# Sigmoids of the six newest tiles at steps 11, 13 and 15, the last rows' x loaded late with its bias at the end, a fifth output buffer, and another late order on ScalarE

## The chip, the cores and the metric

The kernel runs on one NeuronCore of a Trainium2 chip. The metric is the device time of one execution in microseconds (us). The kernel before took 541.62 us (median of 3 runs, 540.72 to 543.06).

## The reference

There are four samples of x and k, each 1024 (time) x 1024 (channels) in float32. In the program's terms (`tf` is one number per sample, made from cond by a sigmoid of a sum):

```
decay = exp(-exp(w)) * (0.5 + 0.5 * tf)
ek    = exp(min(k, 30));  ekv = ek * k;  euk = exp(min(u + k, 30))
nf, df = forward scans over time:  a = a * decay + ekv,  b = b * decay + ek
nb, db = the same scans backward
wkv   = sigmoid(x) * (nf + nb - ekv + euk * k) / max(df + db - ek + euk, 1e-8)
y     = wkv * (0.8 + 0.2 * tf)
out   = x + y @ (sign(weight) * mean|weight| per output row).T + bias
```

The key and the value of the recurrence are the same tensor k; x is needed twice, once under the sigmoid and once as the residual of the output.

## The kernel before

**Tiles and steps.** A tile is one sample by 128 channels, turned so that the channels lie on the 128 partitions and time is the free dimension: 4 samples x 8 tiles = 32 tiles. The loop over `n` from 0 to 31 is written once per engine as `step`, and the engines meet through semaphores only (`done(engine, name, n)` waits until operation `name` of tile `n` is complete; operations of one engine run in the order written).

**One tile's way.** SP loads k (L243) and x (L216). TensorE turns k into the PSUM tensor kT (`k_turn`). ScalarE makes the two exponentials (`exps`, L526 and L527). VectorE clamps (L717), makes value and own (L720, L721), runs two forward scans (L694), the backward scan of the numerator (L708), then the gate of the tile before (L737), then the backward scan of the denominator and den (L742). One step of VectorE goes from one L717 to the next. A step later ScalarE takes the logarithm and the exponential of minus it (`inverse`, L558 and L560), GpSimd multiplies (L314), ScalarE makes "two" (L595), GpSimd multiplies again (L323), VectorE gates with the sigmoid of x that TensorE has turned into sT (`s_turn`, L737), and GpSimd multiplies by the numerator (L330). Two steps later the result is split into a high and a low half in float16 (`halves` on ScalarE, `low_half` on GpSimd, L284). The numerator gets its own term by an accumulating DMA that GpSimd issues (L305; L335 for the last tile).

**The sigmoids.** In every even step ScalarE loads the sigmoid table, applies the sigmoid to the x tiles n and n + 1 in their own buffers (L620; three buffers `x_nat`), and loads the table of exp and log again (L622).

**The product with the weight.** The weight is reduced to signs in the first eight steps. For the first three samples the products run feature by feature: 48 units `u` (an output tile m = u // 2 and a half of time), each of 16 matmuls of 512 columns into one of two PSUM banks (L371). `made(n)` says how many units TensorE has made by the end of step n: two per step at first, then 4, 3, 3, 3, 3 in steps 25 to 29. ScalarE evacuates a unit (`evac`, L537), TensorE turns it back (`turned`, L349 into yT; it is written behind the next unit), and ScalarE copies it into an output buffer `o_nat` (`y_copy`, L546). `clear(lo, hi)` is evac of u followed by y_copy of u - 1; `cleared(n)` says how many units are evacuated by the end of step n. The order within ScalarE's step is: inverse, halves, a first piece of clears, "two", exps, one more clear, the sigmoids in even steps, the rest of the clears. The output tile m lies in buffer m % NO, with NO = 4; y_copy waits until the store of the tile that lay there before has landed. When both halves of a tile are copied, GpSimd issues a DMA that adds x from HBM (`residuals`, L297), and SP stores it (L226). Tiles 21, 22 and 23 are summed and stored behind the loop.

**The last sample** is multiplied the other way round (`across`, L407), with time on the partitions: 16 results of 128 x 512, for which VectorE scales (L769) and adds (L773) x plus bias. That x lies in rows of 4 KB in eight buffers `x_tail(q)`: six of `x_end`, loaded by SP in steps 2 to 7, and the two k buffers, loaded in steps 30 and 31 (L220). The bias is added to them by accumulating DMAs from GpSimd (`biases`, L290): six in steps 3 to 8, two behind everything. SP stores the rows (L263, L267) behind the stores of tiles 21 to 23 in its program.

**Queues.** SP's DMAs run on queue q1, GpSimd's (all that accumulate) on queue q0; both are served by the same 16 DMA engines.

Of the kernel before, what the change touches and what calls it, by code (L numbers as in the profile page):

```python
# [22 lines left out]
P = 128  # L23
# [18 lines left out]
def bi_wkv_binary_ffn(nc, x, k, cond, w, u, weight, bias, out):  # L42
# [7 lines left out]
    LAG = CT + 1  # L50
    TD = cond.shape[1]
    LAST = N - CT
    NO = 4
    NX = 3
    assert T == C and NH == 2 and CT == 8 and N == 32

# [2 lines left out]
    def made(n):  # L59
        return 0 if n < LAG else 2 * LAST if n > N - 4 else MORE.get(n, 2 * (n - LAG + 1))  # L60

    def cleared(n):
        return 0 if n < LAG else 2 * LAST if n >= N - 2 else made(n) if made(n) == made(n - 1) else made(n) - 1

    copied = {u - 1: n for n in range(N) for u in range(cleared(n - 1), cleared(n))}
    copied[2 * LAST - 1] = N - 2
# [7 lines left out]
    def tile_of(a, n):  # L74
        return a.rearrange("b (q p) (c f) -> b c p q f", p=P, f=P)[n // CT, n % CT]

    with ExitStack() as ctx:
# [6 lines left out]
        def sem(name):  # L84
            return ctx.enter_context(nc.semaphore(name))
# [69 lines left out]
        o_out, res_in = ([sem(f"{a}{p}") for p in range(NO)] for a in ("o_out", "res_in"))  # L155
        t_in = [sem(f"t_in{q}") for q in range(TT)]
        b_in = [sem(f"b_in{q}") for q in range(TT)]
        s_tail = sem("s_tail")

        st = {a: sem("d_" + a) for a in (  # L160
            "kT", "expE", "expU", "sig", "sT", "clamp", "val", "own", "Fd", "Fn", "starts", "yd", "yn", "den",
            "ln", "rec", "chk", "two", "inv", "gate", "base", "hi", "hib", "lo",
            "prod", "ev", "yT", "yc", "abs", "sgn", "wT", "wTc", "orow", "orow_sb", "early", "early_sb", "nat", "joined",
            "scaled", "res", "last_chk", "last_inv", "last_base", "last_lo")}

        def seed(eng, *steps):
# [3 lines left out]
        def done(eng, a, n):  # L170

            eng.wait_ge(st[a], n + 1 + SEED)
# [14 lines left out]
        def run(step):  # L187

            for n in range(N):
# [2 lines left out]
        bank = [prod[:, 0, :], prod[:, 1, :], kT[:, 0:H], kT[:, H:T],  # L192
                yT[:, :, :].rearrange("p q f -> p (q f)"), cols[:, :], sT[:, 0:H], sT[:, H:T]]

        def x_tail(q):
            return x_end[:, q, :] if q < TT - 2 else k_nat[q - TT + 2][:, :, :].rearrange("p q f -> p (q f)")

        def natural(a, q):
            return a[B - 1, q * P:(q + 1) * P, :]
# [3 lines left out]
        @block.sync  # L203
        def _(sp):
            for p in range(NO):
                sp.sem_inc(o_out[p], 16)
            for i, a in enumerate((w, u, bias)):
                sp.dma_start(rows[i * CT:(i + 1) * CT, :], a.rearrange("(c p) -> c p", p=P)).then_inc(s_par, 16)
            sp.dma_start(cond4[:, :], cond).then_inc(s_cond, 16)
            sp.wait_ge(s_par, 48)  # L210
            sp.wait_ge(s_cond, 16)
            sp.dma_start(k_nat[1][:, :, :], tile_of(k, 1)).then_inc(k_in[1], 16)

            def load_x(n):

                sp.dma_start(x_nat[n % NX][:, :, :], tile_of(x, n)).then_inc(x_in[n % NX], 16)  # L216

            def load_tail(q):

                sp.dma_start(x_tail(q), natural(x, q)).then_inc(t_in[q], 16)  # L220

            def stores(n):
                for m in summed(n):

                    sp.wait_ge(res_in[m % NO], m // NO * 16 + 16)
                    sp.dma_start(tile_of(out_, m), o_nat[m % NO][:, :, :]).then_inc(o_out[m % NO], 16)  # L226

            load_x(0)
            load_x(1)

            def step(n, p, wt, nxt, nxt3, mid, low, out):
                if wt:

                    done(sp, "sgn", n - 2)
                    done(sp, "abs", n - 2)
                    sp.dma_start(w_nat[p][:, :], weight.rearrange("(o p) i -> o p i", p=P)[n])\
                      .then_inc(w_in[p], 16)
                if n == 0:
                    load_x(2)
                if nxt3:  # L240

                    done(sp, "kT", n + 1)
                    sp.dma_start(k_nat[1 - p][:, :, :], tile_of(k, n + 3)).then_inc(k_in[1 - p], 16)  # L243
                if mid and n + 2 < N:

                    done(sp, "sT", n - 1)
                    load_x(n + 2)
                if 2 <= n < TT:
                    load_tail(n - 2)
                if n >= N - 2:  # L250

                    done(sp, "kT", n)
                    load_tail(TT - N + n)
                stores(n)

            out_ = out
            run(step)
            for n in range(N, added[-1] + 1):
                stores(n)
            for q in range(TT - 1):  # L260

                done(sp, "res", 2 * q + 1)
                sp.dma_start(natural(out_, q), x_tail(q)).then_inc(s_tail, 16)  # L263
            for h in range(NH):

                done(sp, "res", 2 * TT - 2 + h)
                sp.dma_start(natural(out_, TT - 1)[:, h * H:(h + 1) * H], x_tail(TT - 1)[:, h * H:(h + 1) * H])\  # L267
                  .then_inc(s_tail, 16)
            for p in range(NO):
                sp.wait_ge(o_out[p], 16 * LAST // NO + 16)  # L270
            sp.wait_ge(s_tail, 16 * TT + 16)

        @block.gpsimd
        def _(pool):
# [12 lines left out]
            def biases(q):  # L287

                pool.wait_ge(t_in[q], 16)
                pool.dma_start(x_tail(q), bias.unsqueeze(0).to_broadcast([P, C]), accum_op=ALU.add)\  # L290
                    .then_inc(b_in[q], 16)
# [8 lines left out]
            def step(n, p, wt, nxt, nxt3, mid, low, out):  # L300
# [14 lines left out]
                first = n % CT == 1  # L315
                if low and first:
                    low_half(n - 2, p)
                if 3 <= n <= TT:
                    biases(n - 3)
                if mid:  # L320

                    done(pool, "two", n - 1)
# [10 lines left out]

            done(pool, "yn", N - 1)
            pool.dma_start(ekv[1], own[1][:, :], accum_op=ALU.add).then_inc(num_in[1], 16)  # L335
            low_half(N - 2, 0)
            for n in range(N, added[-1] + 1):
                residuals(summed(n))
            biases(TT - 2)
            biases(TT - 1)  # L340

        @block.tensor
        def _(pe):
# [14 lines left out]

            def s_turn(n):

                done(pe, "sig", n)
                done(pe, "gate", n - 1)
                turn(lambda q: sT[:, q * P:(q + 1) * P], TT, lambda q: x_nat[n % NX][:, q, :],
                     ident[:, :]).then_inc(st["sT"], 1)

            def product(u, tiles):
# [143 lines left out]
        def _(act):  # L510
# [70 lines left out]
            def step(n, p, wt, nxt, nxt3, mid, low, out):  # L581
                if mid:
                    inverse(n - 1, 1 - p)
                if low:

                    done(act, "base", n - 2)
                    halves(n - 2, p)
                if out:
                    clear(cleared(n - 1), made(n - 1))
                if n == N - 1:  # L590
                    early_out(2)
                if mid:
# [3 lines left out]
                                   scale=-HI_SCALE * LO_GAIN, bias=two[:, 0:1]).then_inc(st["two"], 1)  # L596
                if n == N - 2:
                    y_copy(2 * LAST - 1)
                if nxt:
                    exps(n + 1, 1 - p)  # L600
                if n == N - 2:
                    early_out(0)
                    early_out(1)
                if out:
                    clear(made(n - 1), min(cleared(n), made(n - 1) + 1))
                if wt:

                    landed(act, w_in, n, p)
# [4 lines left out]
                    done(act, "wT", n - 2)  # L613
                    act.activation(s_nat[p], w_nat[p][:, :], ACT.Sign, scale=TINY_GAIN, bias=tiny[:, 0:1])\
                       .then_inc(st["sgn"], 1)
                if p == 0:

                    for i in range(2):
                        x_landed(act, n + i)
                        act.activation(x_nat[(n + i) % NX][:, :, :], x_nat[(n + i) % NX][:, :, :], ACT.Sigmoid)\  # L620
                           .then_inc(st["sig"], 1)
                    act.preload_act_table_set("natural_log_exp_and_others")  # L622
                if wt:

# [5 lines left out]
                    act.copy(orow[:, 0:H], prod[:, 0, :])  # L630
                    act.copy(orow[:, H:C], prod[:, 1, :]).then_inc(st["orow_sb"], 1)  # L631
                if out:
                    clear(made(n - 1) + 1, cleared(n))

            run(step)

# [162 lines left out]
```

## Time and profile before

| | |
|---|---|
| time, median of 3 | 541.62 us |
| the profiled execution's own time | 540.41 us |
| its span, first to last instruction | 538.7 us |
| VectorE busy | 502.4 us (93%) |
| ScalarE busy | 388.7 us (72%) |
| TensorE matmuls busy | 370.4 us (69%) |
| GpSimd busy | 363.1 us (67%) |
| DMA moved | 92.65 MB, 172 GB/s in the mean |

All durations come from one profiled execution. PE is TensorE, DVE VectorE, ACT ScalarE, POOL GpSimd, SP the engine that issues most DMAs. A share of busy time is an average over the whole span and says nothing about which engine sets the length of one stretch; for that the stretches are looked at one by one.

### The profile page before, as it was taken

To read this page: it belongs to the slowest core of one execution; us is meant where nothing else is said; L and a number is where in the kernel's file an instruction comes from. 1 tells how busy PE (TensorE), PEld (TensorE's weight loads), DVE (VectorE), ACT (ScalarE), POOL (GpSimd) and SP (SyncE) were. 2 spreads that over 40 slices of the span, in tenths; PEclk is the share of its full clock that TensorE was granted. 3 is DMA by queue.
4 is the path that set the end of the run, shared out by engine and by line. 5 is a ranking of instruction groups with operands and counts; after the bars stand their busy time and mean duration, and the time that the engine had idled before them with its cause. 6 is when DMAs were issued, how large, how long until landed. Compare 5 with 4: busy or idle time off the path is not lost.

```text
span 538.7 us, 5362 instructions
## 1 busy us (share of the span) xinstructions
PE 370.4 (69%) x1797; PEld 213.2 (40%) x1803; DVE 502.4 (93%) x379; ACT 388.7 (72%) x424; POOL 363.1 (67%) x194
## 2 busy tenths in 40 slices
PE   2333323333768787877877988967498988597897
PEld 1222222222434453444444454544255545343443
DVE  4999999999999999999999999999999899697694
ACT  2869798897859696977969797969769797583100
POOL 0057777767767778777867887788766877466500
PEclk9995555655697977977978898977799999797999
DMA  6756778786645888998888888889959788653994
GB/s 190 201 143 177 184 191 219 196 231 158 141 117 120 184 175 186 195 193 170 166 175 164 179 178 182 176 177 195 195 84 189 173 180 180 133 81 75 123 312 190
DMA packets 125923, 92.65 MB, mean 172 GB/s; under 512 B 2860, under 2 KB 117576, under 8 KB 125896
## 3 DMA queue, kind: packets, MB, share of 16 engines
q0 software_dynamic: 30720, 33.56, 39.5%
q1 hardware_dynamic: 93096, 57.70, 36.2%
q10 hardware_dynamic: 2080, 1.05, 0.7%
q8 instruction: 15, 0.25, 0.2%
q14 instruction: 12, 0.10, 0.1%
HBM read 58.74 MB, written 16.78 MB: 140 GB/s over the span
## 4 chain that ended last, share of the span: by engine, by line
DVE 43%; issue 18%; PE 15%; POOL 13%; ACT 8%; DMA 2%; SPq 0%; DVEq 0%; POOLq 0%; ACTq 0%
DVE pair L694 15%; DVE pair L708 9%; PE prod L371 5%; DVE wkv L737 4%; DVE pair L720 4%; DVE own L721 4%; POOL wkv L314 4%; POOL wkv L323 3%; POOL acts L284 3%; PE sT L407 3%; DVE pair L717 3%; DVE euk L742 2%; PE prod L407 2%; ACT rec L558 1%; PE yT L349 1%
## 5 line engine op out<-in xcount | busy, mean ns | idle before, releaser
L371 PE MATMUL prod<-acts,sgn 128*128 128x512 f16 x768 | 195.7, 413 | 7.0 <-ACT orow L631 3.1
L708 DVE TENSOR_TENSOR_SCAN pair<-cols,y_start,pair 128x1024 f32<-128x1024 f32 x64 | 150.1, 2347 | 1.3 <-DVE y_start L700 0.2
L694 DVE TENSOR_TENSOR_SCAN pair<-cols,pair 128x1024 f32<-128x1024 f32 x64 | 142.9, 2274 | 0.0
L371 PEld LDWEIGHTS prod<-acts,sgn 128*128 128x128 f16 (+1 forms) x768 | 81.1, 106 | 103.2 <-issue 28.4
L314 POOL TENSOR_TENSOR wkv<-euk,rec 128x1024 f32<-128x1024 f32 x31 | 77.6, 2503 | 38.0 <-ACT rec L560 38.0
L323 POOL TENSOR_TENSOR wkv<-wkv,rec 128x1024 f32<-128x1024 f32 x31 | 73.5, 2371 | 43.8 <-ACT wkv L595 43.8
L349 PE MATMUL kT<-ident,k_nat 128*128 128x128 f32 x256 | 46.8, 343 | 71.2 <-DVE own L721 71.2
L558 ACT ACTIVATE rec<-euk,lnb 128x1024 f32<-128x1024 f32 x32 | 36.8, 1149 | 61.6 <-DVE euk L742 61.6
L330 POOL TENSOR_TENSOR wkv<-wkv,pair 128x1024 f32<-128x1024 f32 x31 | 73.1, 2358 | 10.4 <-DVE wkv L737 10.1
L284 POOL TENSOR_TENSOR acts<-wkv,rec 128x1024 f16<-128x1024 f32 x31 | 74.0, 2388 | 4.7 <-ACT rec L569 4.7
L349 PEld LDWEIGHTS kT<-ident,k_nat 128*128 128x128 f32 x256 | 38.2, 179 | 77.7 <-issue 77.7
L297 POOL DMA_DIRECT2D o_nat<-in_x_dram x24 | 37.9, 1660 | 26.5 <-DVE pair L717 26.5
L349 PE MATMUL yT<-ident,y_fm 128*128 128x128 f32 x192 | 34.9, 313 | 24.5 <-ACT o_nat L546 23.9
L349 PE MATMUL sT<-ident,x_nat 128*128 128x128 f32 x256 | 41.3, 315 | 5.3 <-ACT x_nat L620 5.3
L742 DVE SCALAR_TENSOR_TENSOR euk<-euk,pair 128x1024 f32<-128x1024 f32 x32 | 43.9, 1371 | 1.1
L537 ACT ACTIVATE y_fm<-prod,bcol,oscale 128x512 f32<-128x512 f32 x48 | 37.2, 776 | 10.5 <-issue 6.3
L737 DVE SCALAR_TENSOR_TENSOR wkv<-wkv,sT 128x1024 f32<-128x1024 f32 x31 | 37.2, 1199 | 7.0 <-POOL wkv L323 7.0
L595 ACT ACTIVATE wkv<-wkv,two 128x1024 f32<-128x1024 f32 x31 | 35.8, 1154 | 6.7 <-POOL wkv L314 6.7
L349 PEld LDWEIGHTS yT<-ident,y_fm 128*128 128x128 f32 x192 | 25.7, 160 | 36.9 <-ACT y_fm L537 22.9
L720 DVE TENSOR_TENSOR pair<-pair,kT 128x1024 f32<-128x1024 f32 x32 | 39.1, 1222 | 1.3 <-ACT euk L527 0.3
L349 PEld LDWEIGHTS sT<-ident,x_nat 128*128 128x128 f32 x256 | 36.0, 165 | 10.9 <-ACT x_nat L620 6.4
L305 POOL DMA_DIRECT2D pair<-own x31 | 27.5, 887 | 18.9 <-DVE pair L708 18.9
(91 smaller groups left out, 524.5 us busy)
## 6 DMA issues: line engine op xcount, KB each, us to landing
x_nat<-in_x_dram SPq DMA_DIRECT2D x32, 512.0 KB, 6.0
pair<-own POOLq DMA_DIRECT2D x32, 512.0 KB, 4.6
k_nat<-in_fside_BxSxS_dram SPq DMA_DIRECT2D x30, 512.0 KB, 4.4
o_nat<-in_x_dram POOLq DMA_DIRECT2D x24, 512.0 KB, 6.2
out_dram<-o_nat SPq DMA_DIRECT2D x24, 512.0 KB, 5.0
y_fm<-in_L_ffn_weight_dram SPq DMA_DIRECT2D x8, 512.0 KB, 7.6
x_end<-in_x_dram SPq DMA_DIRECT2D x6, 512.0 KB, 8.9
x_end<-in_L_ffn_bias_dram POOLq DMA_DIRECT2D x6, 512.0 KB, 6.9
```

The lines of the kernel that those rows point to most:

```text
L284: pool.tensor_tensor(acts[:, 1, n % (2 * CT), :], wkv[p][:, :], rec[p][:, :], ALU.subtract)\
L314: pool.tensor_tensor(W, euk[1 - p][:, :], R, ALU.mult).then_inc(st["chk"], 1)
L323: pool.tensor_tensor(W, W, R, ALU.mult).then_inc(st["inv"], 1)
L330: pool.tensor_tensor(W, W, ekv[1 - p], ALU.mult).then_inc(st["base"], 1)
L349: ins = pe.transpose(dst(q), what(q), one)
L371: ins = pe.matmul(prod[:, h, :], view[:, c, m % CT * P:m % CT * P + P], acts[:, part, m // CT % 2 * CT + c, h * H:(h + 1) * H], start=(par ...
L558: act.activation(rec[p][:, :], euk[p][:, :], ACT.Ln, bias=lnb[:, 0:1]).then_inc(st["ln"], 1)
L694: dve.tensor_tensor_scan(buf, d, buf, 0.0, ALU.mult, ALU.add).then_inc(st["F" + kind], 1)
L708: dve.tensor_tensor_scan(buf[:, ::-1], d, buf[:, ::-1], y_start[:, i:i + 1], ALU.mult, ALU.add)\
L720: dve.tensor_tensor(V, E, kT[:, :], ALU.mult).then_inc(st["val"], 1)
L737: dve.scalar_tensor_tensor(W, W, HI_SCALE * LO_GAIN / DEN_MIN, sT[:, :], ALU.min, ALU.mult)\
L742: dve.scalar_tensor_tensor(U, U, E30, E, ALU.min, ALU.add).then_inc(st["den"], 1)
```

## The change

Seven edits:

- The x tiles 26 to 31 are loaded into the six buffers of `x_end` in steps 4 to 9, and their sigmoids are applied in steps 11, 13 and 15, two in each, with the two table loads. The sigmoids of even steps stay for tiles below 26 only. Where TensorE turns them, it waits for a semaphore of their own.
- x for the last rows is loaded in steps 24 to 29, when the buffers come free: rows 0 to 2 into the three `x_nat`, 3 to 5 into the first three of `x_end`, 6 and 7 into the k buffers as before. Each load waits for sT of the step before.
- All eight bias DMAs stand at the end of GpSimd's program: three ahead of `low_half(30)`, five behind it, and the residuals of tiles 21 to 23 behind these.
- There are five output buffers instead of four.
- `cleared(25)` is 34 instead of 35, so that unit 34 is evacuated in step 26 and not at the end of step 25. The other entries of `CLEARED` are what the rule gave before.
- In steps 26 to 29 ScalarE clears one unit ahead of "two", one between "two" and the exponentials, then (in step 26 only) one behind them, and the rest at the end of the step.
- The final waits of SP count the stores per buffer.

```diff
-    NO = 4
+    NO = 5
+    SOON = N - 6
+    CLEARED = {25: 34, 26: 38, 27: 41, 28: 44, 29: 47}
+
     def cleared(n):
-        return 0 if n < LAG else 2 * LAST if n >= N - 2 else made(n) if made(n) == made(n - 1) else made(n) - 1
+        if n < LAG or n >= N - 2:
+            return 0 if n < LAG else 2 * LAST
+        return CLEARED.get(n, made(n) if made(n) == made(n - 1) else made(n) - 1)
...
+        def x_of(n):
+            return x_end[:, n - SOON, :].rearrange("p (q f) -> p q f", q=TT) if n >= SOON else x_nat[n % NX][:, :, :]
+
         def x_tail(q):
-            return x_end[:, q, :] if q < TT - 2 else k_nat[q - TT + 2][:, :, :].rearrange("p q f -> p (q f)")
+            if 3 <= q < TT - 2:
+                return x_end[:, q - 3, :]
+            a = x_nat[(q + 2) % NX] if q < 3 else k_nat[q - TT + 2]
+            return a[:, :, :].rearrange("p q f -> p (q f)")
...
-                if mid and n + 2 < N:
+                if mid and n + 2 < SOON:
 
                     done(sp, "sT", n - 1)
                     load_x(n + 2)
-                if 2 <= n < TT:
-                    load_tail(n - 2)
+                if 4 <= n < 10:
+                    sp.dma_start(x_of(SOON + n - 4), tile_of(x, SOON + n - 4)).then_inc(s_soon, 16)
+                if LAST <= n < N - 2:
+
+                    done(sp, "sT", n - 1)
+                    load_tail(n - LAST)
...
-                if 3 <= n <= TT:
-                    biases(n - 3)
...
             pool.dma_start(ekv[1], own[1][:, :], accum_op=ALU.add).then_inc(num_in[1], 16)
+            for q in range(3):
+                biases(q)
             low_half(N - 2, 0)
+            for q in range(3, TT):
+                biases(q)
             for n in range(N, added[-1] + 1):
                 residuals(summed(n))
-            biases(TT - 2)
-            biases(TT - 1)
...
-                done(pe, "sig", n)
+                if n < SOON:
+                    done(pe, "sig", n)
+                else:
+                    pe.wait_ge(st["soon"], n - SOON + 1)
...
+                sooner = min(made(n - 1), cleared(n - 1) + 1)
                 if out:
-                    clear(cleared(n - 1), made(n - 1))
+                    clear(cleared(n - 1), sooner)
...
+                if n > LAST + 1:
+                    clear(sooner, min(sooner + 1, cleared(n)))
+                    sooner += 1
                 if nxt:
                     exps(n + 1, 1 - p)
...
                 if out:
-                    clear(made(n - 1), min(cleared(n), made(n - 1) + 1))
+                    later = max(sooner, min(cleared(n), made(n - 1) + 1))
+                    clear(sooner, later)
...
-                if p == 0:
+                if p == 0 and n < SOON:
 
                     for i in range(2):
                         x_landed(act, n + i)
-                        act.activation(x_nat[(n + i) % NX][:, :, :], x_nat[(n + i) % NX][:, :, :], ACT.Sigmoid)\
-                           .then_inc(st["sig"], 1)
+                        act.activation(x_of(n + i), x_of(n + i), ACT.Sigmoid).then_inc(st["sig"], 1)
+                    act.preload_act_table_set("natural_log_exp_and_others")
+                if n in (11, 13, 15):
+
+                    for i in range(n - 11, n - 9):
+                        act.wait_ge(s_soon, 16 * (N - SOON))
+                        act.activation(x_of(SOON + i), x_of(SOON + i), ACT.Sigmoid).then_inc(st["soon"], 1)
                     act.preload_act_table_set("natural_log_exp_and_others")
...
                 if out:
-                    clear(made(n - 1) + 1, cleared(n))
+                    clear(later, cleared(n))
```

## Rows read from the trace of the kernel before

**Rows 1.** Busy time per step, steps 26 to 31; columns: stretch, length, engines, clock, DMA.

```profile
392.78:408.79 16.01, 16.01 (x91) 9.24 (x90) 15.57 (x11) 13.77 (x16) 11.77 (x6) 1.00 0.78 163
408.79:426.06 17.27, 15.81 (x89) 9.02 (x88) 15.57 (x12) 13.41 (x17) 11.74 (x6) 1.00 0.73 153
426.06:440.77 14.71, 13.10 (x71) 7.00 (x69) 14.50 (x12) 14.48 (x16) 11.86 (x6) 1.00 0.86 178
440.77:456.02 15.25, 12.43 (x71) 7.28 (x72) 14.84 (x11) 11.57 (x15) 11.73 (x6) 1.00 0.83 174
456.02:476.48 20.46, 14.39 (x68) 7.59 (x68) 15.55 (x12) 12.39 (x14) 11.81 (x6) 0.83 0.51 104
476.48:492.87 16.39, 12.28 (x52) 5.48 (x52) 15.60 (x11) 8.18 (x9) 11.71 (x6) 0.87 0.54 96
```

**Rows 2.** Timeline of ScalarE: start, us; in brackets idle before and its releaser.

```profile
186.41 1.15 ACT L558 ACTIVATE rec<-euk,lnb 128x1024 f32<-128x1024 f32 x1 [5.18 <-DVE euk L742]
...
201.12 1.16 ACT L558 ACTIVATE rec<-euk,lnb 128x1024 f32<-128x1024 f32 x1 [0.57 <-DVE euk L742]
```

**Rows 3.** Timeline of ScalarE in steps 27 and 31.

```profile
411.50 1.16 ACT L558 ACTIVATE rec<-euk,lnb 128x1024 f32<-128x1024 f32 x1
...
416.82 1.16 ACT L595 ACTIVATE wkv<-wkv,two 128x1024 f32<-128x1024 f32 x1
...
478.89 1.15 ACT L558 ACTIVATE rec<-euk,lnb 128x1024 f32<-128x1024 f32 x1
```

**Rows 4.** Waits, 392 to 493: total us, times, longest.

```profile
ACT o_nat L546 <- DMA out_dram<-o_nat: 7.7, 2, 5.7
```

**Rows 5.** Bias DMAs on GpSimd (L290): duration ns min/median/max, first and last start.

```profile
L290 POOL DMA_DIRECT2D x_end<-in_L_ffn_bias_dram x6: 853/867/879, 58.5 to 131.4; - x6
L290 POOL DMA_DIRECT2D k_nat<-in_L_ffn_bias_dram x2: 2916/3073/3230, 502.5 to 503.1; - x2
```

**Rows 6.** Timeline of TensorE in step 26.

```profile
396.71 0.60 PE L349 MATMUL yT<-ident,y_fm 128*128 128x128 f32 x4
397.15 3.62 PE L371 MATMUL prod<-acts,sgn 128*128 128x512 f16 x16
400.60 1.04 PE L349 MATMUL sT<-ident,x_nat 128*128 128x128 f32 x8
```

**Rows 7.** Timeline of VectorE in steps 27 and 28.

```profile
423.96 2.17 DVE L742 SCALAR_TENSOR_TENSOR euk<-euk,pair 128x1024 f32<-128x1024 f32 x1
...
436.13 1.20 DVE L737 SCALAR_TENSOR_TENSOR wkv<-wkv,sT 128x1024 f32<-128x1024 f32 x1
...
439.62 1.23 DVE L742 SCALAR_TENSOR_TENSOR euk<-euk,pair 128x1024 f32<-128x1024 f32 x1
```

**Rows 8.** Timeline of GpSimd in step 27 and at the loop's end.

```profile
422.69 2.37 POOL L330 TENSOR_TENSOR wkv<-wkv,pair 128x1024 f32<-128x1024 f32 x1
...
491.73 0.88 POOL L335 DMA_DIRECT2D pair<-own  x1
497.26 2.60 POOL L284 TENSOR_TENSOR acts<-wkv,rec 128x1024 f16<-128x1024 f32 x1 [4.65 <-ACT rec L569]
```

**Rows 9.** The page, DMA issues: kind, count, KB each, us to landing.

```profile
pair<-own POOLq DMA_DIRECT2D x32, 512.0 KB, 4.6
```

**Rows 10.** DMA queues, 504 to 512: packets, MB, share of 16 engines.

```profile
q0 software_dynamic: 2596, 1.42, 140.8%
```

**Rows 11.** DMA queues, 522 to 528.

```profile
q1 hardware_dynamic: 699, 2.46, 102.4%
```

**Rows 12.** DMA queues, 513 to 518.

```profile
q0 software_dynamic: 208, 0.73, 73.1%
q1 hardware_dynamic: 846, 0.43, 31.7%
```

**Rows 13.** The page, DMA queues over the whole span.

```profile
q0 software_dynamic: 30720, 33.56, 39.5%
q1 hardware_dynamic: 93096, 57.70, 36.2%
```

More of the change, by code:

```diff
@@ L157, in bi_wkv_binary_ffn @@
         b_in = [sem(f"b_in{q}") for q in range(TT)]
-        s_tail = sem("s_tail")
+        s_tail, s_soon = sem("s_tail"), sem("s_soon")
         st = {a: sem("d_" + a) for a in (
@@ L162, in bi_wkv_binary_ffn @@
             "ln", "rec", "chk", "two", "inv", "gate", "base", "hi", "hib", "lo",
-            "prod", "ev", "yT", "yc", "abs", "sgn", "wT", "wTc", "orow", "orow_sb", "early", "early_sb", "nat", "joined",
+            "prod", "ev", "yT", "yc", "abs", "sgn", "wT", "wTc", "orow", "orow_sb", "early", "early_sb", "soon", "nat", "joined",
             "scaled", "res", "last_chk", "last_inv", "last_base", "last_lo")}
@@ L269, in _ @@
             for p in range(NO):
-                sp.wait_ge(o_out[p], 16 * LAST // NO + 16)
+                sp.wait_ge(o_out[p], 16 * len(range(p, LAST, NO)) + 16)
             sp.wait_ge(s_tail, 16 * TT + 16)
@@ L359, in s_turn @@
             def s_turn(n):
-                done(pe, "sig", n)
+                if n < SOON:
+                    done(pe, "sig", n)
+                else:
+                    pe.wait_ge(st["soon"], n - SOON + 1)
                 done(pe, "gate", n - 1)
-                turn(lambda q: sT[:, q * P:(q + 1) * P], TT, lambda q: x_nat[n % NX][:, q, :],
+                turn(lambda q: sT[:, q * P:(q + 1) * P], TT, lambda q: x_of(n)[:, q, :],
                      ident[:, :]).then_inc(st["sT"], 1)
```

## The prediction

> **What bounds the kernel now.** The step table comes first [rows 1]: one line is one step of the loop over the 32 tiles, from one clamp (L717) to the next, with each engine's busy time. VectorE is busy 14.50 of 14.71 us in step 28, and steps before 26 have the same length (186.41 to 201.12, [rows 2]): its recurrence is the bound, and a step can't be shorter than 14.71 us. Steps 26, 27, 29, 30 and 31 take 16.01, 17.27, 15.25, 20.46 and 16.39 us, together 11.8 us over that floor (1.3 + 2.56 + 0.54 + 5.75 + 1.68). That is all the loop can give back. Behind the loop come 45.8 us (492.87 to 538.7), in which TensorE makes the last sample's products, VectorE scales and adds them, and DMA stores them.
>
> Who makes those steps long is read from ScalarE. In an early odd step it idles 5.18 us before the logarithm L558; in an even one, with two sigmoids and two table loads, 0.57 [rows 2]. So a sigmoid pair costs 4.61 us. From step 25 on, when three or four product units are cleared per step, that no longer fits: the log of step 27 starts at 411.50, 2.7 us behind the step's start, that of step 31 at 478.89, 2.4 behind [rows 3]. GpSimd waits for it, and VectorE's gate (L737) for GpSimd's L323. In addition ScalarE's copies into the four output buffers waited 7.7 us in two places for a store, 5.7 of them in step 30 [rows 4].
>
> **The change part by part.**
> *Sigmoids.* Three pairs leave steps 26, 28 and 30 (3 x 4.61 = 13.8 us of ScalarE) and go into steps 11, 13 and 15, as odd as those with 5.18 idle [rows 2]. 5.18 - 4.61 leaves 0.57, what even steps live with, so five steps in a row stay at 14.7: cost 0. Were the cover short, VectorE would lose the shortfall, at most some tenths three times, since GpSimd and the gate behind have slack too. Number of table loads: unchanged.
>
> *Loads and biases in the first steps.* SP issues six 512 KB loads at steps 4 to 9 instead of 2 to 7, GpSimd six bias DMAs fewer at 0.87 us of issue each [rows 5]. VectorE-bound stretch: 0. The late loads of x for the final outputs stand in SP's program exactly where the loads of tiles 26 to 31 stood, behind the same wait (sT of the step before), with equal bytes: 0.
>
> *Five buffers.* Tile 23 now waits for the store of tile 18, a whole step earlier; both waits of [rows 4] go. Late next there: the y copy's own transpose, below 1 us.
>
> *ScalarE's late order, step by step.* Here one stall is made. Before, ScalarE evacuated unit 34 at the end of step 25, ahead of the log. Now the log starts at 392.9 and the evacuation comes behind it. From the log to "two" (L595) with one unit cleared between them ScalarE takes 5.3 us (411.50 to 416.82, [rows 3]): evacuation of 34 and copy of 33 end at 392.9 + 5.3 = 398.2. TensorE's transpose of unit 34, which began at 396.71 [rows 6], and unit 36 behind it start 1.7 late (398.4). TensorE is busy all of step 26 [rows 1], so this isn't made up: the turn of x (sT), 400.60 before, now 402.3, ready at 403.3. VectorE's gate wants it 10.07 us into a step (436.13 - 426.06, [rows 7]), at 402.85: 0.5 late. GpSimd, 1.3 us earlier than before, is on time. Step 26 ends at 408.1 instead of 408.79.
> Step 27: units 36 and 37 are late with TensorE. Unit 37 is ready at 408.0, its evacuation and copy end at 409.3, and only then the log: 409.3 instead of 411.50, still 1.2 behind the step. 5.3 us later, at 414.6, "two" starts and ends at 415.8 (1.16, [rows 3]), GpSimd's L323 runs to 418.2 (2.37, as L330 in [rows 8]), just when the gate wants it (408.1 + 10.07). Its L330 behind L284 ends at 422.9, while VectorE's den (L742) starts at 421.7. Before, such an L742 took 2.17 us instead of 1.23 and ended 1.07 after L330 (422.69 + 2.37 = 425.06 against 426.13) [rows 7, 8]. So it ends at 423.95, and step 27 takes 15.8.
> Steps 28 to 31: log at 423.95 without sigmoids behind it; TensorE needs per step three units at 3.45 us (397.15 to 400.60) and 0.44 for each transpose (396.71 to 397.15) and two turns of 1.04 [rows 6], 13.8 us, under 14.71. ScalarE was busy 14.48 us in step 28 [rows 1], without sigmoids 14.48 - 4.61 = 9.9. All four fit. Loop end 423.95 + 4 x 14.71 = 482.7 instead of 492.87: **10.2 us gained**. Ends: 11.8 if unit 34 costs nothing; about 5 if TensorE's lateness is passed on once per step, or its clock, 1.00 in steps 26 to 29 [rows 1], falls to half in one of them (a unit would take 6.9).
>
> The Trainium skill (SBUF — State Buffer, "SBUF: two separate sides") says that VectorE with two SBUF inputs and GpSimd take a shared port for a whole instruction, and the other waits. By it L742 ends 1.07 after L330, as the trace has it; were the port shared by halves, step 27 would be 0.35 shorter.
>
> *The end.* All eight biases are now issued behind the last pair DMA: three, then low_half(30), then five, and only then the residuals of tiles 21 to 23. Two things hang on them.
> (a) low_half(30) waited 4.65 us for ScalarE and began at 497.26, behind L335, which ended at 492.6 [rows 8]. Three issues at 0.87 [rows 5] are 2.6: they fit with 2 us to spare. At the 3.07 us of the two that came in a crowd [rows 5] they'd be 9.2 and low_half 4.6 late. Those two stood behind three residuals and these behind one pair DMA: I take 0, and if they took 3.07 the end would be no later than the queue's plus about 1 (528.5 + 4.6 = 533.1).
> (b) The queue. The residuals sit behind eight biases, and SP stores no final row before tile 23 is summed and stored. Prices of a 0.524 MB transfer: residuals, 1.42 MB of q0 in 8 us [rows 10]: 2.95. Final stores, 2.46 MB in 6 us [rows 11]: 1.28. In the five us in which biases and tile stores ran together, 0.73 and 0.43 MB [rows 12], so 1.39 b + 0.82 s = 5: with s between 1.28 and 2.95, b is 2.84 to 1.85; I take s = 1.7, nearer to the other store, and b = 2.6. The sum for 8 b + 3 s is 25.9, between 23.7 and 26.6. The last pair DMA is issued at 491.73 - 10.2 = 481.5 and lands 4.6 us later [rows 9], at 486.1. Then 25.9 + 3 x 2.95 + 8 x 1.28 = 45.0: 531.1, and about 1 us of landing: **532**. TensorE and VectorE alone would end at 538.7 - 10.2 = 528.5. So the queue takes back 3.5. The biases themselves are in time: the n-th lands at 486.1 + 2.6 n, the fourth at 496.5, wanted by VectorE about 505.
>
> Sum against the profiled execution: span 538.7 to 532, 540.41 to 533.7. The median shown is 541.62, 1.2 above it; 541.62 - 6.7 = **535**.
>
> The Trainium skill (DMA: Bandwidth & Descriptors, "Queues, rings and completion order") has each DMA engine take turns between its queues packet by packet. Were that even, the stores of tiles 21 and 22 would be done inside q0's run, and after it the engines would idle some 2 us until the last tile's store starts: 534. The trace shows q1 with 0.43 of 1.16 MB [rows 12], so something is left over to fill that hole; I stay at 532.
>
> **Rivals.**
> *Full gain:* the queue runs beside TensorE and isn't last; span 528.5, time 531.4. For: the DMA share of 0.54 in step 31 [rows 1], room for the biases; against: the bytes add up to 532.
> *Half the loop's gain:* TensorE, full in steps 26 and 27 [rows 1], passes each late clear on; loop gain about 5. Queue and end shift alike: span 537, time 540. For: each step's first unit waits for a copy behind the log, exp and halves. Against: 0.9 us to spare per step from 28 on.
> *Slower, by the accumulate queue:* place, from the last pair DMA to the last store. Price by the queues' shares of the whole span [rows 13]: q0 39.5% of 538.7 for 33.56 MB is 3.3 us a transfer, q1 36.2% for 57.70 MB 1.8. Then 11 x 3.3 + 11 x 1.8 = 56 instead of 45: end at 543.3, time 546. It decides from 51.4 on. Against: packet times overlap, shares over 100% [rows 10], so this counts doubly.
> *It doesn't do what it says:* steps 26 to 31 are long for TensorE alone and moving the sigmoids frees nothing; only the 5.7 us wait goes, and the queue's 3.5 eat most: time 539 to 541. Against: the log late by 2.4 in step 31, where TensorE isn't full.
>
> **How the numbers follow.** Forecast (533 to 537) 0.50, full gain 0.15, half 0.17, nothing in it 0.09, slower queue 0.09. Low 530.5 takes in the full gain, high 541 the half gain and part of the next. About 0.5%, 2.7 us, is what can be told from no change. Faster (under 538.9): 0.50 + 0.15 + most of the half and a little beyond, 0.80. Same: 0.11. Slower: 0.09.
>
> **What would show it.** Steps 28 to 31 at 14.7 us; steps 26 and 27 at 15.3 and 15.8; L546 without waits for a store; L558 on time from step 28; TensorE's transpose of unit 34 at 398.4. In the end low_half(30) released by ScalarE and not by the bias issues; the residuals of 21 to 23 landing behind all biases, about 516; final stores issued in a row from about 517, and DMA instead of TensorE last. Wrong if low_half waits for issues, if step 11, 13 or 15 is above 14.72, or if steps 28 to 30 still wait for TensorE.

## The result and the profile after

The changed kernel takes 535.13 us (median of 4 runs, 534.35 to 536.63), against 541.17 for the kernel before in the same comparison: a ratio of 0.9886, 95% interval 0.9852 to 0.992. The forecast was 535.0 and faster. The profiled execution took 535.11 us with a span of 533.4; 532 was forecast for the span.

The table of busy time per step (step, length, then busy us and count of TensorE's matmuls, weight loads, VectorE, ScalarE, GpSimd; granted clock, DMA share, GB/s) is the counterpart of [rows 1]:

```profile
392.15:407.55 15.40, 14.54 (x83) 8.27 (x81) 14.61 (x12) 10.72 (x13) 11.84 (x6) 1.00 0.65 119
407.55:423.35 15.80, 15.80 (x90) 9.09 (x89) 15.57 (x11) 12.10 (x15) 11.74 (x6) 1.00 0.94 215
423.35:438.05 14.70, 14.70 (x83) 8.49 (x82) 14.49 (x11) 10.85 (x13) 11.85 (x6) 1.00 0.85 181
438.05:452.97 14.92, 14.92 (x90) 9.08 (x87) 14.51 (x11) 10.73 (x13) 11.84 (x6) 1.00 0.79 177
452.97:467.68 14.71, 11.25 (x46) 6.22 (x47) 14.50 (x11) 9.98 (x12) 11.85 (x6) 0.77 0.72 144
467.68:482.46 14.78, 13.60 (x70) 7.08 (x71) 14.57 (x11) 5.83 (x6) 12.06 (x8) 1.00 0.59 106
```

Step 26 is 15.40, step 27 is 15.80, and of the four behind them three are at the floor and step 29 is 0.2 over it. The loop ends at 482.46 instead of 492.87: 10.4 us, of which 0.6 lies ahead of step 26 (it begins at 392.15 instead of 392.78) and was not forecast. Most of that is step 21, which takes 14.70 us instead of 15.20; its cause is open.

TensorE's timeline in step 26, beside [rows 6], has the pause that was forecast ahead of the transpose of unit 34:

```profile
397.83 0.63 PE L364 MATMUL yT<-ident,y_fm 128*128 128x128 f32 x4 [0.86 <-ACT o_nat L564]
398.29 3.62 PE L389 MATMUL prod<-acts,sgn 128*128 128x512 f16 x16
401.75 1.04 PE L364 MATMUL sT<-ident,x_nat 128*128 128x128 f32 x8
```

x is turned at 401.75 instead of 400.60. Both are later than before, as forecast, but by 1.1 us and not by the 1.7 of the forecast (398.4 and 402.3).

ScalarE's logarithms in the timeline around the new places of the sigmoids (start, length; idle before it in brackets), at the starts of steps 10 to 13, belong to [rows 2]. The idle time before each is that at the end of the step before: 5.10 for step 9, which has no sigmoids, and 0.56 or 0.57 for steps 10, 11 and 12.

```profile
156.87 1.15 ACT L576 ACTIVATE rec<-euk,lnb 128x1024 f32<-128x1024 f32 x1 [5.10 <-DVE euk L770]
171.58 1.15 ACT L576 ACTIVATE rec<-euk,lnb 128x1024 f32<-128x1024 f32 x1 [0.56 <-DVE euk L770]
186.29 1.15 ACT L576 ACTIVATE rec<-euk,lnb 128x1024 f32<-128x1024 f32 x1 [0.56 <-DVE euk L770]
201.01 1.15 ACT L576 ACTIVATE rec<-euk,lnb 128x1024 f32<-128x1024 f32 x1 [0.57 <-DVE euk L770]
```

Steps 10 to 16 now have a pair each, seven in a row; the idle time is 0.56 or 0.57 us after each of them, and the spacing stays at 14.71. The early sigmoids cost nothing.

The behaviour at the shared port in step 27, VectorE's den and GpSimd's last product (timelines), as in [rows 7, 8]:

```profile
421.25 2.18 DVE L770 SCALAR_TENSOR_TENSOR euk<-euk,pair 128x1024 f32<-128x1024 f32 x1
```

```profile
419.98 2.37 POOL L343 TENSOR_TENSOR wkv<-wkv,pair 128x1024 f32<-128x1024 f32 x1
```

419.98 + 2.37 = 422.35, and den ends 1.08 behind that, at 423.43 (before, 1.07).

At the end, GpSimd's timeline, the counterpart of [rows 8]:

```profile
481.32 0.90 POOL L348 DMA_DIRECT2D pair<-own  x1
481.92 2.97 POOL L305 DMA_DIRECT2D x_nat<-in_L_ffn_bias_dram  x3
486.86 2.60 POOL L299 TENSOR_TENSOR acts<-wkv,rec 128x1024 f16<-128x1024 f32 x1 [1.97 <-ACT rec L587]
489.41 2.61 POOL L305 DMA_DIRECT2D x_end<-in_L_ffn_bias_dram  x3
491.07 2.71 POOL L305 DMA_DIRECT2D k_nat<-in_L_ffn_bias_dram  x2
492.14 6.40 POOL L312 DMA_DIRECT2D o_nat<-in_x_dram  x3
```

GpSimd has issued the three biases 1.97 us before low_half(30) is released, by ScalarE as before. The DMA queues (packets, MB, share of 16 engines) from 486 to 505, when q0 carries biases alone, and from 522 to 530, when q1 carries the final rows:

```profile
q0 software_dynamic: 1061, 3.88, 105.6%
```

```profile
q1 hardware_dynamic: 939, 3.21, 101.3%
```

For transfers of 0.524 MB, 3.88 MB in 19 us is 2.57 us a bias, and 3.21 MB in 8 us is 1.31 us a store. SP's DMA issues (start, length over the group, count) and the last operation of VectorE (timelines):

```profile
511.07 6.84 SPq L237 DMA_DIRECT2D out_dram<-o_nat  x3
517.96 3.05 SPq L278 DMA_DIRECT2D out_dram<-x_nat  x3
521.05 3.65 SPq L278 DMA_DIRECT2D out_dram<-x_end  x3
524.74 1.24 SPq L278 DMA_DIRECT2D out_dram<-k_nat  x1
526.02 2.48 SPq L282 DMA_DIRECT2D out_dram<-k_nat  x2
```

```profile
526.73 0.69 DVE L801 TENSOR_TENSOR k_nat<-sT,k_nat 128x512 f32<-128x512 f32 x1
```

The last add of the kernel before:

```profile
535.47 0.69 DVE L773 TENSOR_TENSOR k_nat<-sT,k_nat 128x512 f32<-128x512 f32 x1
```

VectorE is done at 527.42, and the span ends 6.0 us later. Before, the last add ended at 536.16, and 2.5 us followed. So 3.5 us of the end now belong to DMA, as forecast. They are the queue's: with VectorE done, the DMA engines are still full (share 1.02 in the stretch 526 to 530), and the last store, issued at 527.45, lands 5.5 us later; before, it took 2.0.

Both ends came 1.4 us later than forecast, the queue's (533.4 instead of 532) and VectorE's (527.4 instead of 526.0). VectorE's is explained by TensorE's timeline: behind low_half(30) stand 28 matmuls

```profile
489.61 7.86 PE L425 MATMUL sT<-sgn,acts 128*128 128x512 f16 x28 [5.14 <-POOL acts L299]
```

which took 6.20 in the kernel before:

```profile
500.01 6.20 PE L407 MATMUL sT<-sgn,acts 128*128 128x512 f16 x28 [1.72 <-POOL acts L284]
```

The granted clock in the stretches 486:492 and 492:496 is 0.80 and 0.88 here, and it was 1.00 in 496:502 and 502:507 there. Before, the stretch at 1.2 GHz lay ahead of this block (0.54 in 490:496); now it falls into it. This doesn't explain the queue's 1.4 us, since the engines were full nearly without a break; that is taken up in the account of the prediction.

### The profile page after: what moved, and what is told of

It is laid out like the page before. It is cut to its first block, busy times and chain, and to the rows that moved or that the text cites. A ratio compares the mean times of both kernels' runs of the same rounds, so it can differ in the third digit from the quotient of the medians.

```text
span 533.4 us, 5364 instructions
## 1 busy us (share of the span) xinstructions
PE 365.5 (69%) x1797; PEld 212.1 (40%) x1803; DVE 498.4 (93%) x379; ACT 388.8 (73%) x424; POOL 363.9 (68%) x194
## 4 chain that ended last, share of the span: by engine, by line
DVE 66%; issue 20%; PE 9%; ACT 2%; POOL 1%; DMA 1%; DVEq 0%; SPq 0%; ACTq 0%; POOLq 0%
DVE pair L722 25%; DVE pair L736 14%; DVE pair L748 7%; DVE wkv L765 7%; DVE own L749 6%; DVE pair L745 4%; PE sT L425 3%; DVE euk L770 2%; PE kT L425 1%; PE prod L425 1%; PE prod L389 1%; DVE y_start L728 1%; PE cols L425 1%; PE yT L425 1%; ACT rec L576 1%
## 5 line engine op out<-in xcount | busy, mean ns | idle before, releaser
L389 PE MATMUL prod<-acts,sgn 128*128 128x512 f16 x768 | 192.7, 408 | 6.1 <-ACT orow L659 3.1
L312 POOL DMA_DIRECT2D o_nat<-in_x_dram x24 | 39.5, 1872 | 26.0 <-DVE pair L745 26.0
L770 DVE SCALAR_TENSOR_TENSOR euk<-euk,pair 128x1024 f32<-128x1024 f32 x32 | 40.3, 1258 | 1.1
L544 ACT ACTIVATE pair<-kT 128x1024 f32<-128x1024 f32 x32 | 32.5, 1017 | 10.7 <-PE kT L364 10.7
L749 DVE SCALAR_TENSOR_TENSOR own<-euk,kT 128x1024 f32<-128x1024 f32 x32 | 38.8, 1213 | 0.0
L364 PE MATMUL sT<-ident,x_nat 128*128 128x128 f32 x208 | 34.2, 319 | 5.3 <-ACT x_nat L643 5.3
```

What stands on the lines that cost most here:

```text
L364: ins = pe.transpose(dst(q), what(q), one)
L389: ins = pe.matmul(prod[:, h, :], view[:, c, m % CT * P:m % CT * P + P], acts[:, part, m // CT % 2 * CT + c, h * H:(h + 1) * H], start=(par ...
L749: dve.scalar_tensor_tensor(own[p][:, :], U, E30, kT[:, :], ALU.min, ALU.mult)\
L770: dve.scalar_tensor_tensor(U, U, E30, E, ALU.min, ALU.add).then_inc(st["den"], 1)
```

## The experiments

Each time is a median, and each ratio is to the kernel before as measured beside it (540.97 us for the first three experiments and the one with the residuals, 540.84 for the others, 541.17 for the changed kernel itself). Two changed kernels are therefore best compared by their ratios. The first clamp comes between 8.9 and 9.9 us in the profiled executions, so lengths of steps say more than spans: a difference of up to 1 us in a span can lie ahead of the loop.

**Five buffers alone.**

```diff
-    NO = 4
+    NO = 5
...
-                sp.wait_ge(o_out[p], 16 * LAST // NO + 16)
+                sp.wait_ge(o_out[p], 16 * len(range(p, LAST, NO)) + 16)
```

> The kernel before with five output buffers and nothing else. Theory: the 7.7 us that ScalarE waited for stores go, step 30 loses its 4.7 us wait and takes 15 to 16 us, steps 26, 27 and 31 stay as long as before (16.0, 17.3, 16.4), because the sigmoids are still there. Since the early biases keep the accumulate queue short, nothing is taken back at the end: span about 533, time about 536, as good as the whole change. Rival (the gain is the sigmoids', the buffer merely shifts ScalarE's wait to the transposes behind it): gain under 2 us, time 540 or more.

Measured: 534.44 us, ratio 0.9886 (0.9865 to 0.9907). One line gives all that the whole change gives. Its steps 26 to 31:

```profile
392.02:407.96 15.94, 15.94 (x91) 9.24 (x90) 15.57 (x11) 13.77 (x16) 11.80 (x6) 1.00 0.79 163
407.96:425.20 17.24, 15.79 (x89) 9.02 (x88) 15.54 (x11) 13.40 (x17) 11.76 (x6) 1.00 0.73 154
425.20:439.91 14.71, 13.13 (x71) 7.00 (x69) 14.50 (x11) 14.47 (x16) 11.87 (x6) 1.00 0.87 179
439.91:455.17 15.26, 14.30 (x84) 8.77 (x85) 14.85 (x12) 11.43 (x15) 11.74 (x6) 1.00 0.82 172
455.17:469.89 14.72, 12.01 (x67) 6.73 (x67) 14.51 (x12) 14.04 (x16) 11.89 (x6) 1.00 0.71 144
469.89:484.61 14.72, 11.91 (x53) 5.63 (x53) 14.51 (x11) 6.27 (x7) 11.78 (x6) 0.88 0.60 107
```

Against [rows 1], step 30 falls from 20.46 to 14.72 and step 31 from 16.39 to 14.72, while both sigmoids and table loads are still in step 30. Step 31 had been expected to stay long. So the late sigmoids of step 30 alone don't make it long. The buffer is worth 5.74 + 1.67 = 7.4 us in the loop. What is left over the floor with five buffers lies in steps 26, 27 and 29: 1.23 + 2.53 + 0.55 = 4.3. Of this, steps 27 and 29 go with the sigmoids (the kernel with ScalarE's old order, below, has 14.71 and 14.91 there, 2.9 us less), and step 26 does not, as is shown there. Behind the loop, where the biases of rows 0 to 5 are not in the queue, VectorE's last add ends at 529.4 and the span at 531.9: there is no DMA tail.

**Four buffers again in the changed kernel.**

```diff
-    NO = 5
+    NO = 4
```

> The changed kernel with four output buffers again. Theory: in step 30 the copy of unit 46 waits for the store of tile 19 until about 463.7 instead of starting at 457.9, 'two' is 5.8 us late, step 30 takes about 20 us; span 538.9 and time 540.5, 5.4 more than the changed kernel: nearly all of the change's net gain is this one buffer. Rival (the early sigmoids carry the gain): under 2 us more.

Measured: 541.28 us, ratio 1.0015 (1.0002 to 1.0027). Without the buffer the change is worth nothing. Steps 29 to 31, and the copy of unit 46 in ScalarE's timeline:

```profile
437.28:453.39 16.11, 12.76 (x73) 7.30 (x72) 15.55 (x11) 11.10 (x14) 11.73 (x6) 1.00 0.76 164
453.39:474.02 20.63, 14.27 (x63) 7.41 (x63) 15.54 (x11) 10.31 (x13) 11.81 (x6) 0.83 0.51 103
474.02:488.81 14.79, 13.60 (x69) 6.98 (x70) 14.58 (x11) 5.83 (x6) 12.06 (x8) 1.00 0.59 106
```

```profile
464.33 0.59 ACT L564 COPY o_nat<-yT 128x512 f32<-128x512 f32 x1 [5.89 <-DMA out_dram<-o_nat]
```

The wait is back at its full size with no sigmoid anywhere near it. The copy starts at 464.33, "two" directly behind it, 6 us late. ScalarE waits for stores three times here, 13.6 us in all, and the loop is 7.1 us longer than with five buffers: 1.2 in step 29 and 5.9 in step 30. Step 31 is not long although step 30 took 20.63 us. As far as these two runs show, it took both, a late step 30 and sigmoids at its end, to make step 31 of the kernel before 1.7 us longer.

**ScalarE's old order in the changed kernel.**

```diff
-    CLEARED = {25: 34, 26: 38, 27: 41, 28: 44, 29: 47}
+    CLEARED = {}
...
-                sooner = min(made(n - 1), cleared(n - 1) + 1)
+                sooner = made(n - 1)
...
-                if n > LAST + 1:
-                    clear(sooner, min(sooner + 1, cleared(n)))
-                    sooner += 1
```

> The changed kernel with ScalarE's clears in the order of before (no CLEARED table, all that is left ahead of 'two'). Theory: the late order is worth nothing: step 26 has the 1.3 us of before (unit 34 ahead of the log, log at +1.4), step 27 is 14.7 to 15 instead of 15.8, because units 36 and 37 aren't 1.7 us late on TensorE: the sum stays within 0.7 us of the changed kernel, 535.1. Rival (the order is what makes the three-unit steps fit without the sigmoids): steps 27 to 29 over 15.5 us each, 2 us or more slower.

Measured: 533.57 us, ratio 0.9864 (0.9849 to 0.9879), by the ratios 1.2 us under the changed kernel. Steps 26 and 27:

```profile
391.58:406.75 15.17, 15.17 (x86) 8.64 (x84) 14.96 (x11) 11.45 (x15) 11.75 (x6) 1.00 0.80 171
406.75:421.46 14.71, 14.71 (x84) 8.46 (x82) 14.50 (x11) 10.82 (x13) 11.84 (x6) 1.00 0.87 182
```

With unit 34 cleared ahead of the logarithm TensorE goes on without a pause, and step 27 is at the floor. Steps 26 to 31 together take 89.0 us instead of 90.3. Of these 1.3 us, 1.1 are step 27.

Step 26 was expected at 16.0 and is 15.17. The reason is TensorE's clock ahead of the step. The unit of 16 matmuls that begins about 4 us ahead of it, in TensorE's timeline of this kernel, of the changed kernel and of the last one below ("Both"):

```profile
387.36 3.62 PE L389 MATMUL prod<-acts,sgn 128*128 128x512 f16 x16
```

```profile
388.35 4.73 PE L389 MATMUL prod<-acts,sgn 128*128 128x512 f16 x16
```

```profile
388.35 4.35 PE L389 MATMUL prod<-acts,sgn 128*128 128x512 f16 x16
```

The granted clock of the stretch 386 to 391 is 0.91, 0.54 and 0.62 in them: the clock rose from 1.2 to 2.4 GHz at different times, also where the programs are the same up to this unit, as in the first and the third. In the old order TensorE is full, so the transpose of unit 34, and with it the step, comes later by what the lower clock cost:

| old order for unit 34 | transpose, us into step 26 | step 26 |
|---|---|---|
| old order in the changed kernel | 3.12 | 15.17 |
| only unit 34 back (next experiment) | 3.19 | 15.26 |
| five buffers alone | 3.86 | 15.94 |
| kernel before | 3.93 | 16.01 |
| both (last experiment) | 4.26 | 16.34 |

In all five the step ends 12.05 to 12.08 us after this transpose starts, with the late sigmoids (third and fourth line) or without them. So the 1.3 us that step 26 had over the floor before were TensorE's clock and not the sigmoids. In the new order the transpose waits for ScalarE and starts 5.68 us into the step in the changed kernel and in the four other kernels that keep this order; where no fall of the clock follows, step 26 takes 15.40 or 15.41 and step 27 15.78 to 15.80. The new order thus costs 1.1 us in step 27, and in step 26 between -0.9 and 0.2, depending on the clock. The difference in time is within the intervals of the two ratios; the steps show it, the medians alone don't.

**Only unit 34 back in step 25.**

```diff
-    CLEARED = {25: 34, 26: 38, 27: 41, 28: 44, 29: 47}
+    CLEARED = {25: 35, 26: 38, 27: 41, 28: 44, 29: 47}
```

> The changed kernel with unit 34 cleared in step 25 again; the clear between 'two' and the exponentials stays. Theory (the late order costs through unit 34, whose transpose comes 1.1 to 1.7 us late on a full TensorE): as with the whole old order, steps 26 and 27 at 15.2 and 14.7, time 533.6. Rival (the clear between 'two' and the exponentials, which waits for its transpose, is what costs): 535.1 as the changed kernel.

Measured: 533.88 us, ratio 0.9873 (0.9853 to 0.9893); steps 26 and 27 take 15.26 and 14.71, as with the whole old order. So it is unit 34 that costs, and the clear between "two" and the exponentials does neither good nor harm.

**Residuals ahead of the five last biases.**

```diff
             low_half(N - 2, 0)
-            for q in range(3, TT):
-                biases(q)
             for n in range(N, added[-1] + 1):
                 residuals(summed(n))
+            for q in range(3, TT):
+                biases(q)
```

> The changed kernel with the residuals of tiles 21 to 23 issued ahead of the five last biases. The bytes are the same; only what SP waits for lands earlier (tile 23 about 503 instead of 517). Theory (the queue's order takes back some 3 to 4 us at the end): the tile stores and the first rows' stores run while TensorE still works, the last store follows VectorE's last add (527.4) by 2.5 us, span about 530, time about 531.7, 3.4 less than the changed kernel. Rival (the 16 DMA engines are full from 484 on, so the sum of bytes sets the end whatever the order): span stays at 532 to 533.4.

Measured: 535.09 us, ratio 0.9887 (0.9871 to 0.9904). The theory falls: the place of the residuals in the queue is worth nothing. SP's timeline:

```profile
498.40 18.17 SPq L237 DMA_DIRECT2D out_dram<-o_nat  x3
516.61 4.43 SPq L278 DMA_DIRECT2D out_dram<-x_nat  x3
```

The first tile store is issued 12.7 us earlier than in the changed kernel, and yet SP reaches the final rows at 516.6 instead of 518.0, because the stores crawl. The queues in the stretch 508 to 512, biases on q0 and tile stores on q1:

```profile
q0 software_dynamic: 200, 0.75, 94.2%
q1 hardware_dynamic: 196, 0.10, 12.2%
```

As many packets on either queue, and 7.5 times the bytes on q0: a bias has packets of 4096 bytes and a tile store of 512. The kernel before shows the same from 513 to 516, while its two last biases and the tile stores run together:

```profile
q0 software_dynamic: 153, 0.56, 93.6%
q1 hardware_dynamic: 152, 0.08, 12.5%
```

The Trainium skill says (DMA: Bandwidth & Descriptors, "Queues, rings and completion order") that each DMA engine goes round between its queues packet by packet. The equal counts agree with it, if a packet of the trace stands for an equal share of a packet of the page, which no run here shows. The engines are full in either order (in the changed kernel their share is 1.0 or more from 484 to 517 and from 520 to 530, and 0.87 between), so the bytes issued behind the loop set the end.

**The six biases left out.** The result lacks the bias in rows 0 to 5 of each eight.

```diff
-            for q in range(3):
-                biases(q)
             low_half(N - 2, 0)
-            for q in range(3, TT):
+            for q in range(TT - 2, TT):
                 biases(q)
...
-                    dve.wait_ge(b_in[q], 16)
+                    dve.wait_ge(b_in[q] if q >= TT - 2 else t_in[q], 16)
```

> The changed kernel without the six bias DMAs for rows 0 to 5 (their bias is left out of the result); the two for rows 6 and 7 stay, ahead of the residuals. Theory now (putting the residuals earlier gave nothing, so it is not the order but the bytes: the 16 engines are full from 484 to 532, and six accumulates of 2.6 us are 15 us of it): the engines are no longer full, VectorE's last add at 526.7 is followed by the last store in 2.5 us, span 529.5, time 531.2. Rival (the end hangs on the 512-byte tile stores, which go one packet per packet of q0): still 532 or more, because two biases and three residuals still stand before them.

Measured: two executions of 530.81 and 533.81 us, ratio 0.9843 (0.981 to 0.9875); the first was profiled, with a span of 529.1. Two further ones took 651 and 1898 us; their cause is open, and they are left out. The profiled one is as the theory says:

```profile
525.87 0.69 DVE L799 TENSOR_TENSOR k_nat<-sT,k_nat 128x512 f32<-128x512 f32 x1
```

VectorE is done at 526.6, and 2.5 us follow. (0.9 us of the shorter span lie ahead of the loop: the first clamp is at 8.91 instead of 9.79.) Taking away six biases (15.4 us of the queue) takes away the DMA tail.

**The six biases in steps 26 to 31.**

```diff
+                if LAST + 2 <= n:
+                    biases(n - LAST - 2)
                 if mid:
 
                     done(pool, "two", n - 1)
...
-            for q in range(3):
-                biases(q)
             low_half(N - 2, 0)
-            for q in range(3, TT):
-                biases(q)
             for n in range(N, added[-1] + 1):
                 residuals(summed(n))
+            biases(TT - 2)
+            biases(TT - 1)
```

> The changed kernel with the six biases issued in steps 26 to 31, between GpSimd's two products, as their x has landed by then, and the last two behind the residuals as before. Theory: GpSimd idles 1.6 us at that place and the DMA share in those steps is 0.5 to 0.86, so six more transfers of 2.6 us cost the loop nothing; the end is that of the kernel without them: span 529.5, time 531.2. Rival (q0 delays the pair DMA of the same step, on which the product with the numerator waits): steps 26 to 31 grow, 534 or more.

Measured: 532.73 us, ratio 0.9849 (0.9822 to 0.9876), 1.5 above what was expected. The runs fall into two groups, 530.5 to 531.6 and 533.9 to 534.8, and the profiled one is of the second. The DMA tail is gone in it (last add done at 529.5, span 532.0), but step 26 takes 17.08 us. TensorE's timeline there:

```profile
397.18 1.08 PE L364 MATMUL yT<-ident,y_fm 128*128 128x128 f32 x4 [2.33 <-ACT o_nat L564]
398.05 4.89 PE L389 MATMUL prod<-acts,sgn 128*128 128x512 f16 x16
```

It is the pause before the transpose of unit 34 again, 2.33 us here instead of 0.86. ScalarE is no later than in the changed kernel (the transpose starts 5.68 us into the step in both), but TensorE was ready earlier, because the unit ahead of the step took 3.62 us and not 4.73. The unit behind the pause takes 4.89 instead of 3.62: the granted clock of the stretch 398.0 to 402.8 is 0.73, so about half of it ran at 1.2 GHz. So the pause that the new order makes may cost a fall of the clock as well; it was seen in this one execution, and the trace shows no wait for a bias in step 26. That the two groups of runs are those with and without that fall was not shown.

**Both: biases in steps 26 to 31, and ScalarE's old order.** The edits of the two experiments together.

> As the one with the biases in steps 26 to 31, and ScalarE's clears in the order of before. Theory: loop ends at 480.6 instead of 482.5, VectorE's last add at about 525.6, last store 2.5 us behind it: span 528.0, time 529.7, 2.1% under the kernel before. Rival as for the other: the loop loses what the end gains, 533.

Measured: 531.23 us (531.05 to 532.55), ratio 0.9833 (0.9814 to 0.9852): 9.6 us under the kernel before, and by the ratios about 2.9 under the changed kernel. Steps 26 and 27:

```profile
392.16:408.50 16.34, 16.34 (x93) 9.44 (x92) 15.57 (x12) 11.98 (x15) 12.59 (x7) 1.00 0.93 188
408.50:423.20 14.70, 14.70 (x83) 8.47 (x82) 14.49 (x12) 10.83 (x13) 12.65 (x7) 1.00 1.05 213
```

The transfers fit in at a DMA share up to 1.06: steps 27 to 31 take 14.70, 14.71, 14.91, 14.71 and 14.8 us, the same as with ScalarE's old order and the biases at the end, and VectorE's last add is followed by 2.5 us. Step 26 is 1.2 us longer than there. That is TensorE's clock again (4.35 us for the unit ahead of the step instead of 3.62, see the table above) and not the bias, after whose issue GpSimd still waits 1.02 us for ScalarE. These 1.2 us and 0.6 ahead of the loop (first clamp at 9.75 instead of 9.15) account for the 1.5 us by which it stays above the 529.7 expected.

## Why the prediction was right, point by point

- **The walk through steps 26 and 27 held.** Forecast 15.3 and 15.8, measured 15.40 and 15.80. The cause was the one named: TensorE's transpose of unit 34 waits for ScalarE (a pause of 0.86 us), and den in step 27 waits for GpSimd. Putting unit 34 back gives 14.71 in step 27. What the forecast didn't see is that step 26's length before depended on when the clock rose, so that the 1.3 us there were not the sigmoids' to give back.
- **Steps 28 to 31 at the floor, loop end at 482.7:** measured 482.46, with 0.2 over the floor in step 29. 0.6 of the 10.4 us came ahead of step 26, so the steps themselves gave 9.8 instead of 10.2.
- **Early sigmoids, early and late loads at no cost:** shown by the 0.56 us left and steps of 14.71.
- **The issues of the first three biases at 0:** right; they ended 1.97 us before low_half(30) was released, "2 us to spare" in the forecast.
- **The queue takes back 3.5 us:** measured 6.0 - 2.5 = 3.5. The prices held, 2.57 for 2.6 and 1.31 for 1.28. But the reason given, that the residuals stand behind eight biases and SP waits for tile 23, was wrong. The sum was in truth one of bytes on full engines, and it came out right for that reason: with the residuals first the end stays, without six biases it goes. That the 3.5 came out to the tenth is luck, since both ends were 1.4 us later than forecast.
- **Span 532, measured 533.4:** from the issue of the last pair DMA to the end the forecast had 50.5 us (481.5 to 532), and it took 52.1 (481.32 to 533.4). That is the queue: the same stretch took 51.9, 51.9 and 51.6 us with four buffers, with the old order and with unit 34 back, while VectorE's last add ended 46.1 us behind that issue in the changed kernel and 47.3, 46.9 and 46.9 in these. So the slower block of 28 matmuls moved VectorE and not the end. Rather more than half of the missing 1.6 us lies ahead of the final stores (the store of tile 23 landed at 517.54 + 4.1 = 521.6, where the sum has 486.1 + 25.9 + 3 x 2.95 = 520.9, from a pair DMA issued 0.2 later); the rest is in the final stores and their landing, for which 1 us was taken.
- **[rows 12] was read as five us in which biases and tile stores ran together.** They did so until 516 only (0.56 and 0.08 MB from 513 to 516); most of the 0.43 MB of q1 came when the biases were nearly done. The equation still gave usable prices, because it shares out the time of full engines. But "the trace shows q1 with 0.43 of 1.16 MB" was no evidence against turns by packets. The 534 that even turns were said to give is in fact nearer to the 533.4 measured, though the idle stretch from which it was worked out is short: a share of 0.87 for 3 us, some 0.4 us instead of 2.
- **The median:** the gain was 6.0 us in the comparison, 6.7 were forecast; 535.0 was met so closely because the kernel before also came out 0.45 lower (541.17 instead of 541.62).
- **What the forecast had wrong is the split between buffer and sigmoids.** It gave the waits for stores 5.7 us in step 30 and took the late logarithm of step 31 as evidence for the sigmoids. The experiments give, in the loop: the buffer 7.4 us (7.1 in the changed kernel), the sigmoids 2.9 (steps 27 and 29), the new order of ScalarE -1.1 in step 27; with the 0.6 by which step 26 is shorter they make the 9.8. The total was right because all parts were in the change. The rival "moving the sigmoids frees nothing" is refuted for the loop, but close to the truth for the whole: what the sigmoids gave, the biases, which had to follow them behind the loop, and the new order took back. Five buffers alone have the same ratio, 0.9886.

## What to carry to other kernels

When a change has several parts, price each alone, and count as consequence what merely follows from an earlier wait: here one buffer, one line, was as much as the whole gain, and the other parts cancelled. A transfer moved out of a stretch with room (a DMA share below 0.9) to the end, where the DMA engines are full, is paid in full, whatever its place in the queue; the same transfers were free in steps 27 to 31. On an engine that is busy all of a step, one clear that comes 1 us later costs about that much in the next. And before a step's length is put down to an edit, look at the granted clock ahead of it: with the same order of work, step 26 took from 15.17 to 16.34 us.

## What the hardware showed that was not expected

- Two queues with packets of different size share the engines by packets: 200 against 196 packets, 0.75 against 0.10 MB in 4 us, and 153 against 152 in the kernel before. Stores in 512-byte packets move about a seventh of the bytes of the accumulates in 4096-byte ones beside them.
- The stretch of lower clock moved with the pauses: the same 28 matmuls took 6.20 us in the kernel before, after a pause of 1.7 us, and 7.86 in the changed one, after 5.1 (7.61 after 4.8 with five buffers alone, 8.92 after 5.0 with the biases in the loop).
- The clock rises at different times in one execution and another (one of each kernel was profiled, and not all on the same chip): 16 matmuls at the same place of the program took 3.62, 4.35 and 4.73 us, and a full TensorE hands the difference on to the next step.
